# A transformer layer on one core: every step of the written order put in new places, and three waits added

## The reference

```python
q = (hidden_states @ Wq)...; k = (hidden_states @ Wk)...; v = (hidden_states @ Wv)...   # head_dim 128, k and v repeated 4 times
scores = jnp.einsum('bhqd,bhkd->bhqk', q, k) * HEAD_DIM ** (-0.5)
probs = jax.nn.softmax(jnp.where(causal[None, None], scores, -jnp.inf), axis=-1)
x = _layernorm(x + jnp.einsum('bhqk,bhkd->bhqd', probs, v)... @ Wo)
base_out = jnp.einsum('bsd,od->bso', x, W_base) + b_base
weights = sparsemax(jnp.einsum('bsd,ed->bse', x, W_router) + b_router)
h = jnp.einsum('bsd,edr->bser', x, lora_A)
x = _layernorm(x + base_out + jnp.einsum('bser,bse,ero->bso', h, weights, lora_B))
```

## Time and profile before

| | us |
|---|---|
| median of 3 runs (lowest, highest) | 674.99 (674.26, 675.61) |
| the profiled execution, its own time | 673.4 |
| its span, first to last instruction | 671.6 |
| PE busy in it, weight loads apart | 653.3 |
| DVE busy | 540.6 |
| ACT busy | 427.3 |
| POOL busy | 258.7 |
| mean granted clock of PE | 0.994 |

### The profile page before, as it was taken

How to read it: one execution, slowest core, us unless ns; L and a number is a source line. 1 busy time by engine, 2 the same in 40 slices (tenths; PEclk the granted TensorE clock), 3 DMA queues, 4 the chain that set the end, 5 groups by cost and what they waited for, 6 DMA issues and landing times.

```text
span 671.6 us, 12091 instructions
## 1 busy us (share of the span) xinstructions
PE 653.3 (97%) x3861; PEld 356.2 (53%) x3861; DVE 540.6 (80%) x1776; ACT 427.3 (64%) x1129; POOL 258.7 (39%) x254
## 2 busy tenths in 40 slices
...
GB/s 299 150 107 137 109 129 154 52 107 52 214 87 75 83 140 138 52 106 55 219 80 79 79 143 135 52 105 58 192 72 84 75 64 181 52 98 34 118 19 93
DMA packets 195408, 71.87 MB, mean 107 GB/s; under 512 B 162320, under 2 KB 187408, under 8 KB 195344
## 3 DMA queue, kind: packets, MB, share of 16 engines
...
q10 hardware_dynamic: 1344, 1.05, 0.6%
...
HBM read 27.02 MB, written 2.10 MB: 43 GB/s over the span
## 4 chain that ended last, share of the span: by engine, by line
PE 91%; DVE 4%; POOL 1%; DMA 1%; issue 1%; ACT 1%; SPq 0%; DVEq 0%; POOLq 0%
PE bank L1309 25%; PE bank L1250 21%; PE bank L1274 12%; PE bank L1293 9%; PE bank L1262 5%; PE bank L1230 4%; PE bank L1299 3%; PE bank L1341 3%; PE bank L1243 2%; PE bank L1233 2%; PE bank L1300 2%; PE bank L1352 1%; PE bank L1223 1%; DVE rowmax L979 1%; DVE qT L958 1%
## 5 line engine op out<-in xcount | busy, mean ns | idle before, releaser
L766 POOL TENSOR_SCALAR raw<-raw,scale_of 128x512 f32<-128x512 f32 (+1 forms) x75 | 120.7, 1610 | 315.3 <-ACT wk L831 189.7
L887 ACT ACTIVATE pr<-pr,mx 128x288 f32<-128x288 f32 (+15 forms) x256 | 131.5, 515 | 66.5 <-DVE mx L1078 65.7
L1250 PE MATMUL bank<-xT,wq 128*128 128x512 f16 x720 | 164.5, 379 | 0.3 <-DVE y L1122 0.3
L1078 DVE CUSTOM_DVE_ANT_0 pr<-bank,mask,back_of 128x32 f32<-128x32 f32 (+15 forms) x256 | 124.9, 495 | 46.0 <-PE bank L1274 45.1
L905 ACT ACTIVATE p<-pr,ri 128x64 f16<-128x64 f32 (+14 forms) x240 | 115.2, 526 | 36.6 <-DVE ri L1089 36.3
L1105 DVE SCALAR_TENSOR_TENSOR p<-pr,ri,p 128x64 f16<-128x64 f32 (+11 forms) x240 | 126.3, 566 | 11.0 <-ACT p L905 10.6
L1274 PE MATMUL bank<-kT,qT 128*128 128x32 f16 (+15 forms) x768 | 122.3, 280 | 2.8 <-DVE qT L958 2.0
L1250 PEld LDWEIGHTS bank<-xT,wq 128*128 128x128 f16 x720 | 69.8, 98 | 80.2 <-DVE y L1122 0.8
L1274 PEld LDWEIGHTS bank<-kT,qT 128*128 128x128 f16 x768 | 67.0, 98 | 55.2 <-issue 3.8
L1309 PE MATMUL bank<-wo_odd,oT 128*128 128x512 f16 x384 | 96.1, 379 | 0.0
L1309 PE MATMUL bank<-wo_even,oT 128*128 128x512 f16 x384 | 96.0, 380 | 0.0
...
## 6 DMA issues: line engine op xcount, KB each, us to landing
raw<-in_wo SPq DMA_DIRECT2D x32, 256.0 KB, 3.7
raw<-in_wq SPq DMA_DIRECT2D x30, 256.0 KB, 3.9
raw<-in_wk SPq DMA_DIRECT2D x8, 256.0 KB, 3.6
raw<-in_wv SPq DMA_DIRECT2D x8, 256.0 KB, 3.8
y<-in_x SPq DMA_DIRECT2D x1, 2048.0 KB, 12.7
pT<-p SPq DMA_TRANSPOSE x128, 3.5
out<-y SPq DMA_DIRECT2D x8, 256.0 KB, 2.0
pT<-in_xT SPq DMA_DIRECT2D x6, 256.0 KB, 7.6
```

The source lines that it names most:

```text
L766: eng.tensor_scalar(whole, raw_of(name, key), scale[0], None, ALU.mult).then_inc(sems["scaled"], 1)
L887: eng.activation(pr[:, t % 2, h, 0:w], pr[:, t % 2, h, 0:w], ACT.Exp, bias=mx[:, k:k + 1], scale=-1.0, accum_out=rs[:, k:k + 1]).then_inc( ...
L1078: eng.tensor_tensor_reduce(out=pr[:, t % 2, h, 0:w], in0=psum("S", t, h)[:, 0:w], in1=mask[:, 0:w], scale=score_scale(t), scalar=BIG, op0= ...
L1250: made = eng.matmul(out, wq[:, g % 2, w, h, c * 128:(c + 1) * 128], xT[:, x, c, b * 512:(b + 1) * 512], start=c == 0 and w + x == 0, stop= ...
```

## The change

All three tables are written in a new order. They hold the same steps as before, and every product keeps its shape. Three waits are added: ACT may write `rl` for rows k only when `hw` of rows k - 2 is made; DVE may write `hw` of rows k only when it has been turned for rows k - 2; and DVE may overwrite the statistics of rows k only when `nmr` of rows k - 4 has been made. Each names a buffer of two (or four) slots. In the new file the line numbers of PE's part are 4 more than before, those of SP, POOL and most of ACT's part 2 less.

```diff
--- before
+++ after
@@ -116,115 +116,113 @@
-    ("fetch", "wo", 0, 3), ("consts",), ("most", "k", 0), ("table",), ("most", "x", 0, 0), ("most", "q", 0), ("most", "x", 0, 2), ("rows",),
...
+    ("fetch", "wo", 0, 3), ("consts",), ("most", "k", 0), ("most", "x", 0, 2), ("most", "q", 0), ("K", 0), ("turn", "A"), ("x", 0, 3), ("x", 0, 2),
...
@@ -921,6 +919,8 @@
                 elif name == "sp":
                     k, = key
                     act.wait_ge(*done("R", k))
+                    if k > 1:
+                        act.wait_ge(*done("hw", k - 2))
                     eng.activation(rl[:, k % 2, :], psum("R", k)[:, 136:272], ACT.Copy).then_inc(sems["ra_half"], 1)
                 elif name == "ht":
                     k, = key
@@ -1164,6 +1164,8 @@
                     dve.wait_ge(*done("sp3", k))
                     eng.tensor_scalar(w8, lg, tau, 0.0, ALU.subtract, ALU.max).then_inc(sems["sp4"], 1)
                     dve.wait_ge(*done("sp4", k))
+                    if k > 1:
+                        dve.wait_ge(*done("ht", k - 2))
                     eng.tensor_tensor(
                         out=hw[:, q, :].rearrange("p (a r) -> p a r", a=8),
                         in0=rl[:, q, 8:136].rearrange("p (a r) -> p a r", a=8),
@@ -1184,6 +1186,8 @@
                     k, = key
                     n = 4 + k % 4
                     dve.wait_ge(*done("F", k))
+                    if k > 3:
+                        dve.wait_ge(*done("nmr", k - 4))
                     eng.bn_stats(st[:, n, :], psum("base", k)[:, :]).then_inc(sems["st2_bn"], 1)
                     dve.wait_ge(*done("st2_bn", k))
                     eng.bn_aggr(mv[:, n, :], st[:, n, :]).then_inc(sems["st2_mv"], 1)
```

More of the change, by code:

```diff
@@ L129 @@
-    ("wo", 0, 2), ("rest", 1, 0), ("Vp", 0, 4), ("inv", 2, 0), ("rest", 1, 1), ("wo", 0, 3), ("S", 3, 0), ("inv", 2, 1), ("Q", 1, 2),
-    ("most", "q", 1), ("bits", ("qk", 1)), ("norm", 2, 1), ("S", 3, 1), ("norm", 2, 0), ("rest", 2, 0), ("wo", 0, 1), ("S", 3, 2), ("Q", 1, 0),
-    ("exp", 3, 0), ("PV", 0, 0), ("wo", 0, 0), ("rest", 2, 1), ("fetch", "wo", 1, 3), ("exp", 3, 2), ("Q_lo", 0, 0), ("exp", 3, 1), ("Q", 1, 3),
[7 rows of a table removed]
-    ("inv", 5, 0), ("wv", 1, 1), ("rest", 4, 1), ("rest", 4, 0), ("inv", 5, 1), ("norm", 5, 1), ("PV", 3, 2), ("turn", ("ov", 1)), ("W", 2, 3),
@@ new lines @@
+    ("most", "o", 1), ("bits", ("ov", 1)), ("wq", 1, 0), ("norm", 4, 0), ("W", 2, 0), ("exp", 5, 0), ("rest", 4, 0), ("exp", 4, 3), ("S", 5, 3),
+    ("inv", 4, 1), ("W", 2, 1), ("wq", 1, 3), ("W", 1, 3), ("exp", 5, 3), ("inv", 5, 0), ("exp", 5, 2), ("W", 2, 2), ("W", 2, 3), ("wq", 1, 2),
+    ("rest", 4, 1), ("inv", 5, 1), ("norm", 4, 1), ("PV", 3, 0), ("turn", ("ov", 1)), ("factor", ("ov", 1)), ("rest", 5, 1), ("norm", 5, 0),
+    ("wv", 1, 0), ("wo", 1, 1), ("rest", 5, 0), ("norm", 5, 1), ("wv", 1, 1), ("PV", 3, 1), ("PV", 3, 2), ("Q", 2, 0), ("wo", 1, 0), ("PV", 3, 3),
@@ new lines @@
+    ("exp", 11, 3), ("exp", 13, 0), ("fetch", "wq", 3, 1), ("S", 12, 3), ("turn", ("ov", 2)), ("W", 9, 2), ("factor", ("ov", 2)), ("rest", 11, 0),
+    ("PV", 10, 0), ("fetch", "wv", 2, 0), ("inv", 11, 1), ("S", 13, 0), ("W", 8, 3), ("S", 13, 1), ("norm", 11, 1), ("rest", 11, 1), ("Q", 4, 0),
+    ("inv", 12, 0), ("most", "v", 2), ("exp", 12, 2), ("S", 13, 2), ("inv", 12, 1), ("exp", 12, 1), ("rest", 12, 0), ("exp", 12, 3), ("Q", 4, 1),
+    ("S", 13, 3), ("PV", 10, 1), ("PV", 10, 2), ("norm", 12, 0), ("Vp", 1, 2), ("norm", 12, 1), ("S", 14, 0), ("rest", 12, 1), ("S", 14, 1),
@@ L202 @@
-    ("norm", 56, 0), ("rest", 56, 0), ("PV", 55, 1), ("exp", 57, 1), ("PV", 55, 2), ("S", 57, 3), ("inv", 57, 0), ("one", 3), ("most", "r", 0),
-    ("S", 58, 0), ("PV", 55, 3), ("S", 58, 1), ("exp", 57, 3), ("most", "b", 0), ("S", 58, 2), ("inv", 57, 1), ("norm", 57, 1), ("S", 58, 3),
-    ("bits", "ffn"), ("Q", 15, 0), ("W", 55, 0), ("exp", 58, 2), ("turn", "ffn"), ("rest", 57, 1), ("norm", 57, 0), ("factor", "ffn"),
-    ("exp", 58, 1), ("rest", 57, 0), ("exp", 58, 3), ("S", 59, 0), ("S", 59, 1), ("exp", 58, 0), ("S", 59, 2), ("inv", 58, 1), ("lb",), ("Q", 15, 3),
@@ L227 @@
-    ("fin", 4), ("fin", 5), ("st2", 7), ("fin", 6), ("fin", 7),
+    ("S", 54, 1), ("S", 54, 0), ("fetch", "wra"), ("S", 54, 2), ("fetch", "lb"), ("Q", 14, 2), ("S", 54, 3), ("exp", 54, 2), ("exp", 54, 0),
+    ("S", 55, 0), ("exp", 54, 3), ("exp", 54, 1), ("fetch", "wb", 0), ("inv", 54, 0), ("S", 55, 1), ("rest", 54, 0), ("exp", 55, 0), ("norm", 54, 0),
+    ("inv", 54, 1), ("most", "l", 0), ("Q", 14, 1), ("PV", 52, 0), ("exp", 55, 2), ("fetch", "wb", 1), ("S", 55, 2), ("exp", 55, 1), ("norm", 54, 1),
[3 rows of a table added]
```

69 lines of the change are left out of this document (35 added, 34 removed), and 117 rows, old and new, of tables (FIRST_STEPS, LAST_STEPS, NEXT_STEPS).

## The result

The changed kernel takes 681.15 us (median of 4 runs, 679.83 to 682.69) against 675.3 for the kernel before (674.26 to 675.73): a ratio of 1.009, 95 % interval 1.0065 to 1.0114. It is 5.9 us slower; the forecast was 5.3 faster, with a range up to 677. In the profiled executions the span goes from 671.6 to 679.3 us. Under 1 % separates the two: in both kernels PE is nearly always busy, and the answer is in a handful of waits.

The account below looks back on a forecast made before the run. PE, busy 653.3 of 671.6 us, was taken as the bound, with losses mostly in the first 84 us. The terms summed to -5.3 us: 674.99 - 5.3 = 669.7 us, whole range 665.5 to 677.

Parts of the forecast that it names:

- (a): Start: without the early dummy exp, ACT's table load comes later and delays turns B and C, +1.05 us.
- (b): First scores: twelve Vp matmuls now stand before them, PE's idle time falls from 1.66 to about 1.25 us, -0.4.
- (c): First score banks: PE work between scores of one bank removes the waits of 0.28 and 0.52 us, -0.8.
- (d): Low clock at 28 to 34 us: half of its 1.68 us goes with the gaps, -0.85.
- (e): Second unit's Q, near 59 us: earlier fetches remove waits of 3.04 and 0.17 and 1.56 us of clock, -4.8.
- (f): Before tile 2's first PV: more products in between remove the 1.79 us wait, -1.8.
- (g): Fetch of y and bb moved from SP's head to before the transposes of tiles 1 and 2: +1.0 us.
- (h): Middle: twelve tight score-bank places cost +1.8 us, 0.49 idle at 500 to 600 us goes, together +1.3.
- (i): Tail: PE's last steps are the same, nothing, within 0.5 us either way.
- (j): Three added waits: none holds anything up, nothing (0 to +0.3 us).
- R2: Rival, slightly slower: y's block holds the transposes by the full 7.8 us, total 676.5 us, chance 0.10.
- R1: Rival, slower: twelve tight score-bank places lose 1.1 us each with DVE 82 % busy, total 681.1 us, chance 0.12.

Follow-up runs that it names:

- e2_rows: Changed kernel with the fetch of bb, br and y put back to the start of SP's list: 673.01 us, ratio 0.9966 to the kernel before.
- e1_first: Changed kernel's new FIRST_STEPS and three waits, with NEXT_STEPS and LAST_STEPS of the kernel before: 673.55 us, ratio 0.9986 to the kernel before.
- e5_first_rows: New FIRST_STEPS with y's fetch back at the start, NEXT_STEPS and LAST_STEPS of the kernel before: 667.28 us, ratio 0.9878 to the kernel before.
- e7_pool: Changed kernel with POOL's two-tensor subtraction exchanged for a scaled copy of one tensor: 673.09 us, ratio 0.996 to the kernel before.
- e4_waits: Kernel before with the three added waits alone: 675.34 us, ratio 1.0005 to the kernel before.
- e12_last: New FIRST_STEPS with y's fetch and the early exp at the start, old NEXT_STEPS, new LAST_STEPS: 666.3 us, ratio 0.9859 to the kernel before.
- e8_queue: Changed kernel with y fetched at the same step but issued by ACT on its own queue: 677.21 us, ratio 1.0018 to the kernel before.
- e3_moves: Changed kernel with four steps of NEXT_STEPS moved to give PE other matmuls where it waited: 676.08 us, ratio 1.0014 to the kernel before.

## Why the prediction was wrong

By its own steps:

- (a), the table load: right in kind. 0.41 at turn B, nothing at turn C; 0.6 to 0.9 us by the traces, 1.05 forecast.
- (b), the first scores: 1.76 us of idle time, 1.25 forecast, 1.66 before. No gain. With POOL's subtraction exchanged it is 0.9.
- (c) and (d), banks of the first scores and the clock at 28 to 34: the waits are gone and the clock is 1.00 there, so all of the 1.68 came back, twice the term.
- (e), the waits for Q at 59 us and the clock behind them: gone, as `e2_rows` shows with 10.00 of 10 us at full clock.
- (f): the 1.79 before tile 2 is gone. The 1.93 at 107 stand before the first PV of tile 6; with the old tables (`e1_first`) nothing over 0.32 stands there, so they count with the new NEXT_STEPS, in (h).
  Together (a) to (f) are well met: -7.6 forecast, and the new head with y put back gave -8.7 (`e5_first_rows`).
- (g), y: **mis-sized by 7.1 us.** I took 1.0 out of a range of 0 to 7.8; `e2_rows` gives 8.1. What failed is y's 6.1 us at 386 GB/s with a transpose landing 3.5 us behind: y took 11.1, though nothing of the start's crowd stood before it (the engines moved 172 to 302 GB/s from 46 to 52 us), and the first transpose took 6.29 us in issuing and landed 11.4 after its start. The upper end, worked out from y's 12.7, was nearer. And I had counted the wait alone. A stop of 4.9 us here was followed by over four microseconds at half clock, and the kernel before had shown the like behind a stop of 3.04.
- (h), the middle: **the step that failed.** Its 1.8 is a price for twelve score banks, and of those the trace has one wait behind the head, 0.27 us at 550.98. The loss is for oT and once a period for qT: 2.03 us a period, 6.1 in three, and 7.6 with what stands around the first (`e1_first` against the changed kernel, the 1.93 of tile 6 among it). I had compared the distance of each pair by a need worked out from undisturbed durations, ACT 0.59 and DVE 0.68, and written "so nothing" for Q; the distance from PV to W I did not work out at all. The need was too low by what DVE may be held up, a POOL subtraction of 1.16 us above all: without it no wait for oT is left (`e7_pool`). A reduction of 2.28 stands ahead of the wait at 295.29, but it does so with the exchange as well, where PE doesn't wait.
- (i) and (j), the end and the waits: nothing, as `e4_waits` and `e12_last` show.

The forecast with these two terms corrected would be 669.7 + 7.1 + (7.6 - 1.3) = 683.1; measured 681.15. Of the rest 1.1 lies in the head, which gave more than (a) to (f) say; 0.9 stays open, about what comparing across the groups can hide. With one of the two terms wrong the forecast would have been 6.3 or 7.1 us off, just inside the stated range; it took both. R2's price (7.8) was nearly right and its chance of 0.10 too low; its mechanism, the order of one queue, is not it by `e8_queue`, where a transpose ahead of y on the other queue was held as well. R1 had the sign of the middle and the wrong bank. They were treated as alternatives, though a loss at y and one in the middle could, and did, come at once.

What the collisions with POOL's subtraction take of DVE's busy time: 10 us in the old order (540.6 to 530.7) and 19.5 in the new (553.6 to 534.1). The old order bears its ten without a wait: with the exchange it is not faster. So neither tightness nor collisions alone cost time here. Moving four steps (`e3_moves`) and removing the collisions (`e7_pool`) each take most of the same waits away.

The Trainium skill, SBUF — State Buffer, Who interferes with whom, says that a DVE instruction with two SBUF inputs contends with a GpSimd instruction that reads SBUF, and calls the contention an exclusive lock. The trace agrees that they contend, and for L766 a stop can last until POOL's instruction is through (1.24 us of L1102). For POOL's instructions that read one tensor it shows shorter stops, at most 0.45 us beside instructions of 1.56 or more, and often none: L1102 took 0.25 beside one, in the rows above.
